# A state space layer over 24 chunks: other places in the order of work for its side matmuls and softplus, and five lent sum units instead of seven

## The chip, the cores and the metric

The kernel runs on one core of a Trainium2 chip. The time is that of one execution on the device, in microseconds (us), as the median of several runs. TensorE does the matmuls and the transposes, VectorE the scans and sums, ScalarE the activations, GpSimd elementwise work, and SyncE issues the DMAs. The engines run on their own and are ordered by semaphores; each engine works through its own list strictly in order.

## The reference, cut to what matters

Four layers follow one another on an input of 4 images, 384 channels, 48 x 48 pixels. Only the first, a state space block after a group norm, is touched. For each image, with L = 2304 pixels as a sequence:

```
xin, z = split(xn @ in_proj_w.T)                   # 768 + 768 channels
xin = silu(conv4(xin) + conv_b)                    # causal, 4 taps
dt, B, C = split(xin @ x_proj_w.T)                 # 24, 16, 16
dt = softplus(dt @ dt_proj_w.T + dt_proj_b)
h = exp(dt * A) * h + dt * B * xin                 # 16 states per channel, a scan along L
y = sum over states(h * C) + xin * D
out = layernorm((y * silu(z)) @ out_proj_w.T)
x = x + out
```

Layers 2 to 4 (an FFT convolution, a sparse 11 x 11 convolution, a gated mixture) are the same in both kernels.

## The kernel before, in words

**Chunks and units.** The sequence of each image is cut into 6 chunks of T = 384 pixels, so there are NCH = 24 chunks. Each chunk needs 96 scans of 384 pixels (16 states x 6 blocks of 128 channels); two share one scan instruction, so a chunk has PAIRS = 48 units. For a unit, TensorE transposes six 128 x 128 blocks of dt*B*x into PSUM (`inputs`, line 451, tiles pw0 and pw1 in turn), ScalarE computes two exponentials exp(dt*A) (line 600) and a copy of the start states (605), and VectorE scans (744). Three units make one state r. TensorE then transposes the states back, six blocks a unit, into the one tile pw2 (`turned`, 462), and VectorE adds them, weighted with C, to an accumulator a_acc (763; 757 for the first state). GpSimd prepares dt*B*x for three units at a time (`scaled`, 882) and keeps the last states (888).

**Lent units.** In the units that the tuple `LENT` names (positions 0 to 47 in a chunk), VectorE does not do the sum: ScalarE copies pw2, weighted, into a_tm12 (614), and GpSimd adds that to a_acc (894). The next `turned` waits until pw2 has been read, by VectorE or by ScalarE.

**Steps.** A chunk's main loop has STEPS = 96 steps n. In even steps are `inputs` and the scan of unit n/2, in odd ones `turned` and the sum of unit (n-1)/2 - 3. So the lent units 20, 22, 24, 26, 38, 41, 43 stand at the odd steps 47, 51, 55, 59, 83, 89, 93. ScalarE's exponentials run LEAD = 7 steps ahead; its lent copy is at the even step after.

**Side work.** Beside chunk k's main loop run chunk k-1's end (`post_*`: transposes of a_acc 344, gate, out-projection 353, layer norm, transposes G 360 and the residual 655) and chunk k+1's start (`pre_*`, `gate_*`: in-projections P 373 and Z 413, causal convolution, x-projection 381, B and C 387, the dt-projection V 394, softplus, transposes T 401). Each is a generator that yields the step at which its next piece is due; `march` issues what is due before the step's main work, in order of these times. On TensorE side work is issued only in odd steps, ahead of that step's `turned`. The times are written by hand: A_AT, O_AT (with O_GAP), LN_AT, G_AT, T_AT, Z_AT, and numbers in the functions. Chunk 0's start runs alone, before the first scan; the last chunk's end runs beside the next layer, with its times times 0.35.

**Banks.** Side matmuls write one of two PSUM banks: ps3 (`S`) or ps2 (`D`). `Turn.claim` makes each new user wait until the last one has been read. In the kernel before, P, B and C, V, T and Z all use S; the a_acc transposes, the out-projection, x-projection and G use D. V's reader on ScalarE is a pair, Abs into dt and Relu into raw (548, 549); then Exp and Ln run over all six blocks at once (552, 556: 128 x 2304), and GpSimd makes dt and dt*x (841, 845).

**DMA order.** SyncE's list has, for each chunk, the store of x of chunk k-1 (waits for the last G operation, v_g) and the reload of its buffer with chunk k+2. In the third chunk of images 0 to 2, VectorE also takes the statistics of the next image from 18 pieces that go through one buffer a_sx (705); 13 of their loads are issued before the store and the reload, 5 behind them.

Of the kernel before, what the change touches and what calls it, by code (L numbers as in the profile page):

```python
# [18 lines left out]
T = 384  # L19
# [344 lines left out]
def pre_pe(e, m, w, S, D, k):  # L364
    s, ps, pd, ident, o = m.s, m["ps3"], m["ps2"], m["g_ident"], k % 2
    for i in range(6):
        for kk in range(CT):
            yield 2.5 + 5.4 * i + 1.6 * kk
            if kk == 0:
                S.claim("a_raw", 6 * k + i + 1)  # L370
                w.wait_ge("p_xn", 3 * (k + 1))
                w.wait_ge("d_w0", 96)
            t = e.matmul(ps[:, 0:T], m["a_WinT"][:, kk, i * 128:(i + 1) * 128], m["a_xn"][:, kk, :], start=kk == 0, stop=kk == 2)  # L373
        t.then_inc(s["pe_P"], 1)
    for j in range(6):
# [48 lines left out]


def stats_pe(e, m, w, D, b):
    yield 89
    D.claim("v_st", GN * b + 24)
    w.wait_ge("v_st", GN * b + 23)
    w.wait_ge("d_c", 32)  # L430
    groups_pe(e, m, m["ps2"], m["a_mv"]).then_inc(m.s["pe_gn"], 1)


def l0_pe(e, m, w, S, D):
    s, ident = m.s, m["g_ident"]
    w.wait_ge("d_c", 32)
    march([stats_pe(e, m, w, D, 0)], 0)
    march([pre_pe(e, m, w, S, D, 0), gate_pe(e, m, w, S, 0)], 0)

    def inputs(k, p):  # L440

        pi = PAIRS * k + p
        g, c = NS * k + p // 3, 2 * (p % 3)
        ps = m[f"pw{pi % 2}"]
        w.wait_ge("p_dbt", g + 1)
        w.wait_ge("v_scan", pi - 1)
        w.wait_ge("v_w", 5)
# [49 lines left out]
def pre_act(e, m, w, k):  # L497
# [42 lines left out]
    for i in range(6):  # L540
        yield 58.4 + 0.8 * i
        w.wait_ge("pe_V", 6 * k + i + 1)
        w.wait_ge("p_cv", 24 * (k + 1))
        if k % NQ < NQ - 1:
            w.wait_ge("p_halo", k + 2)
        w.wait_ge("p_dtx", 6 * (k - 1))
        w.wait_ge("a_exp", 3 * PAIRS * (k - 1))
        e.activation(dt[:, i, :], ps[:, 0:T], ACT.Abs, bias=pv[:, i, 5:6])
        e.activation(raw[:, i, 3:T + 3], ps[:, 0:T], ACT.Relu, bias=pv[:, i, 5:6]).then_inc(s["a_v"], 1)
    yield 64.5  # L550
    w.wait_ge("a_v", 6 * (k + 1))
    e.activation(dt[:], dt[:], ACT.Exp, scale=-1.0).then_inc(s["a_sp"], 1)
    yield 67
    w.wait_ge("a_sp", 2 * k + 1)
    w.wait_ge("p_const", 3)
    e.activation(dt[:], dt[:], ACT.Ln, bias=m["a_one"][:, 0:1]).then_inc(s["a_sp"], 1)
# [74 lines left out]
def post_dve(e, m, w, k):  # L631
# [185 lines left out]
def pre_pool(e, m, w, k):  # L817
# [111 lines left out]
def l0_sp(e, m, d, w):  # L929
# [37 lines left out]

POST = 0.35
# [1213 lines left out]
```

## Time and profile before

| | us |
|---|---|
| median of 3 runs | 5353.92 (5347.02 to 5355.37) |
| the profiled execution | 5347.93, span 5346.1 |
| state space stage, first scan to last sum | 3210.2 |
| VectorE busy over the span | 4381.3 (82%) |
| TensorE busy over the span | 4686.3 (88%) |
| ScalarE, GpSimd busy over the span | 3070.4 (57%), 2970.7 (56%) |

All rows come from one execution; times are from the span's start. A row's length is that of the instruction; the next one on the same engine can start some 0.1 us before it ends, so what an instruction costs in a full row of work is the distance between starts. A value in brackets is the engine's idle time before it and what ended it. A 384-column matmul in fp32 shows as two instructions (x2), one transposed set as six. "PEclk" is the granted TensorE clock as a share of 2.4 GHz; 0.5 is its lower level, 1.2 GHz.

### The profile page before, as it was taken

Reading aid. Unit: us, or ns where it says so; the run is one execution under the profiler, and the core shown is the slowest. Engines: PE = TensorE matmul, PEld = TensorE weight load, DVE = VectorE, ACT = ScalarE, POOL = GpSimd, SP = SyncE. Lnnn points to the kernel's source line nnn. Section 1 sums busy time; section 2 is a strip of 40 time slices with the busy share of each in tenths; the row PEclk is TensorE's granted clock in tenths of the full one; section 3 lists DMA queues with packets and bytes.
Section 4 is the critical chain, followed back from the end, with each engine's and each line's share of the span. In section 5 each row is a group of like instructions: output and inputs, shape, how many; then the busy total and the mean of one; then the engine's idle time right before and its main releaser. Section 6 shows DMA issues by size and latency. Waiting matters only on the chain.

```text
span 5346.1 us, 78656 instructions
## 1 busy us (share of the span) xinstructions
PE 4686.3 (88%) x28623; PEld 3835.5 (72%) x28623; DVE 4381.3 (82%) x4965; ACT 3070.4 (57%) x6391; POOL 2970.7 (56%) x3552
## 2 busy tenths in 40 slices
PE   4888888888888888888888886779998899999999
PEld 2666666666666666666666665446877799999999
DVE  1999999999999999999999999677677765665555
ACT  3777777777777777777777774333332223333333
POOL 3776777777777777777777775456554520000000
PEclk8999999999999999999999999889797988999999
DMA  2001000001000001000000001110201021112110
GB/s 78 1 13 33 10 10 10 10 11 35 10 10 10 10 11 35 10 10 10 10 10 10 10 5 44 44 32 20 92 20 41 26 72 53 54 51 60 45 60 29
DMA packets 96933, 148.64 MB, mean 28 GB/s; under 512 B 5748, under 2 KB 93604, under 8 KB 96548
## 3 DMA queue, kind: packets, MB, share of 16 engines
q1 hardware_dynamic: 96548, 143.63, 8.4%
q8 instruction: 227, 3.72, 0.3%
q14 instruction: 158, 1.29, 0.1%
HBM read 101.00 MB, written 42.61 MB: 27 GB/s over the span
## 4 chain that ended last, share of the span: by engine, by line
PE 50%; issue 15%; DVE 15%; POOL 12%; ACT 7%; DMA 1%; POOLq 0%; DVEq 0%; SPq 0%; ACTq 0%
PE pw L1776 8%; PE pw L1763 6%; PE pw L462 6%; PE pw L451 6%; DVE a_h L744 5%; POOL a_dBT L882 4%; PE ps L413 3%; PE ps L353 3%; DVE b_cv L1393 3%; PE ps L373 2%; DVE a_acc L763 2%; PE ps L1763 2%; POOL a_xin L834 2%; POOL a_acc L894 2%; PE pw L1176 2%
## 5 line engine op out<-in xcount | busy, mean ns | idle before, releaser
L744 DVE TENSOR_TENSOR_SCAN a_h<-a_dA,pw 128x771 f32<-128x771 f32 x1152 | 2015.7, 1752 | 125.6 <-PE pw L451 124.6
L600 ACT ACTIVATE a_dA<-a_dt,a_Aneg 128x384 f32<-128x384 f32 x2304 | 1345.5, 607 | 155.0 <-DVE a_h L744 150.1
L462 PEld LDWEIGHTS pw<-g_ident,a_h 128*128 128x128 f32 x6912 | 786.6, 142 | 619.8 <-DVE a_acc L763 267.1
L882 POOL TENSOR_SCALAR a_dBT<-a_dtxT,a_BC 128x768 f32<-128x768 f32 x1152 | 1026.2, 909 | 300.7 <-PE pw L451 216.6
L462 PE MATMUL pw<-g_ident,a_h 128*128 128x128 f32 x6912 | 983.1, 279 | 227.5 <-DVE a_acc L763 158.1
L451 PE MATMUL pw<-g_ident,a_dBT 128*128 128x128 f32 x6912 | 958.9, 276 | 4.8 <-POOL a_dBT L882 4.8
L763 DVE SCALAR_TENSOR_TENSOR a_acc<-pw,a_BC,a_acc 128x768 f32<-128x768 f32 x912 | 915.3, 1004 | 52.5 <-PE pw L462 48.1
L451 PEld LDWEIGHTS pw<-g_ident,a_dBT 128*128 128x128 f32 x6912 | 806.5, 143 | 6.5 <-POOL a_dBT L882 5.5
L834 POOL TENSOR_TENSOR a_xin<-a_xin,a_tm 128x384 f32<-128x384 f32 x432 | 433.3, 1003 | 34.2 <-ACT a_tm L521 9.0
L1887 DVE TENSOR_TENSOR d_hf<-d_hf,d_wb 128x384 f32<-128x384 f32 x288 | 159.1, 557 | 312.4 <-ACT d_hf L1819 300.2
L894 POOL TENSOR_TENSOR a_acc<-a_acc,a_tm 128x768 f32<-128x768 f32 x168 | 307.4, 1830 | 171.1 <-ACT a_tm L614 170.2
L413 PE MATMUL ps<-a_xn,a_WinT 128*128 128x384 f32 x864 | 345.5, 502 | 30.7 <-ACT a_sz L577 15.1
L373 PE MATMUL ps<-a_xn,a_WinT 128*128 128x384 f32 x864 | 350.8, 490 | 10.2 <-ACT a_raw L509 5.1
L353 PE MATMUL ps<-a_WoT,a_sz 128*128 128x384 f32 x864 | 338.9, 489 | 23.1 <-POOL a_sz L793 23.1
L1819 ACT ACTIVATE d_hf<-pw,d_b 128x384 f32<-128x384 f32 x216 | 125.2, 580 | 352.0 <-PE pw L1763 352.0
L1279 ACT ACTIVATE b_xh<-ps 128x384 fp32r<-128x384 f32 x144 | 70.6, 490 | 415.5 <-PE ps L1132 415.5
L1776 PE MATMUL pw<-e_hh,c_W2h 128*128 128x384 f32 x864 | 288.8, 334 | 1.7 <-DVE e_hl L1892 1.7
L1776 PE MATMUL pw<-e_hl,c_W2h 128*128 128x384 f32 x864 | 288.6, 334 | 0.0
L1776 PE MATMUL pw<-e_hh,c_W2l 128*128 128x384 f32 x864 | 288.6, 334 | 0.0
L1591 POOL TENSOR_SCALAR b_xw<-b_x,b_sw,b_bw 128x384 f32<-128x384 f32 x288 | 223.1, 796 | 114.8 <-PE pw L1132 114.7
L1575 POOL TENSOR_TENSOR b_cv<-b_cv,b_tm 128x768 f32<-128x768 f32 x96 | 196.3, 2045 | 131.4 <-ACT b_tm L1260 127.0
L521 ACT ACTIVATE a_tm<-a_raw,a_pv 128x384 f32<-128x384 f32 x432 | 259.5, 601 | 7.4 <-POOL a_xin L834 7.3
(228 smaller groups left out, 9377.7 us busy)
## 6 DMA issues: line engine op xcount, KB each, us to landing
d_wb<-cw SPq DMA_DIRECT2D x24, 768.0 KB, 5.7
a_xs<-in_x SPq DMA_DIRECT2D x24, 576.0 KB, 3.9
x<-a_xs SPq DMA_DIRECT2D x24, 576.0 KB, 3.0
b_x<-x SPq DMA_DIRECT2D x24, 576.0 KB, 4.4
b_xs<-x SPq DMA_DIRECT2D x24, 576.0 KB, 5.0
e_xs<-x SPq DMA_DIRECT2D x24, 576.0 KB, 3.8
out<-e_xs SPq DMA_DIRECT2D x24, 576.0 KB, 5.8
a_sx<-in_x SPq DMA_DIRECT2D x54, 192.0 KB, 2.3
```

The lines of the kernel that those rows point to most:

```text
L353: t = e.matmul(pd[:, 0:C], m[f"a_sz{o}"][:, j, tb * 128:(tb + 1) * 128], m["a_WoT"][:, j, :], start=j == 0, stop=j == 5)
L373: t = e.matmul(ps[:, 0:T], m["a_WinT"][:, kk, i * 128:(i + 1) * 128], m["a_xn"][:, kk, :], start=kk == 0, stop=kk == 2)
L413: t = e.matmul(ps[:, 0:T], m["a_WinT"][:, kk, DI + i * 128:DI + (i + 1) * 128], m["a_xn"][:, kk, :], start=kk == 0, stop=kk == 2)
L451: t = e.transpose(ps[:, at:at + 128], m[f"a_dBT{g % 2}"][:, tb, (c + h) * 128:(c + h + 1) * 128], ident[:])
L462: t = e.transpose(m["pw2"][:, c * 128:(c + 1) * 128], m[f"a_h{g % 2}"][:, c // 2, first_col(c) + tb * 128:first_col(c) + (tb + 1) * 128], ...
L600: e.activation(dA[:, first_col(c):first_col(c) + T], m[f"a_dt{k % 2}"][:, c, :], ACT.Exp, scale=m["a_Aneg"][:, c, n:n + 1]).then_inc(s["a_ ...
L744: e.tensor_tensor_scan(m[f"a_h{g % 2}"][:, p % 3, :], m[f"a_dA{pi % NDA}"][:], m[f"pw{pi % 2}"][:, COL:COL + PAIR], 1.0, ALU.mult, ALU.add ...
L763: e.scalar_tensor_tensor(out=acc, in0=ps, scalar=cs, in1=acc, op0=ALU.mult, op1=ALU.add).then_inc(s["v_acc"], 1)
L834: e.tensor_tensor(xin[:, i, :], xin[:, i, :], m[f"a_tm{pr % NTM}"][:], ALU.add).then_inc(s["p_cv"], 1)
L882: t = e.tensor_scalar(m[f"a_dBT{g % 2}"][:, tb, :], m[f"a_dtxT{o}"][:, tb, :], m[f"a_BC{o}"][:, tb, n:n + 1], 1.0, ALU.mult, ALU.mult)
L1763: t = e.matmul(hidden3(m, hi), m[f"c_{A}"][:, kk, col], m[f"e_{B}{o}"][:, kk, :], start=kk == z == 0, stop=kk == z == 2)
L1776: t = e.matmul(ps, m[f"c_{A}"][:, i, col], m[f"e_{B}{u % 2}"][:, i, :], start=x == 0 and i == 0 and z == 0, stop=x == 3 and i == z == 2, s ...
```

## The change

- The times of TensorE's side work are written as slots, odd steps that hold at most about two matmuls; the due time says which. X-projection goes from 47 .. 53 to 48.5 .. 52.6, V is spread from 58 .. 62 to 56.6 .. 66.5, Z's eighteen matmuls get a time each, G moves from 60 .. 66 to 70.6 .. 84.7, and T from 78.6 .. 87.6 to 72.5 .. 84.6. The last out-projection block begins at 39.4 instead of 40.2.
- V, T and Z take the banks S and D in turn, as V_BANK, T_BANK and Z_BANK say.
- Softplus's Exp and Ln run on three blocks at a time, the first half between the two halves of V; GpSimd's dt and dt*x follow each half, from step 66 instead of 69.
- LENT has five units: 20, 26, 30, 38, 43, at the odd steps 47, 59, 67, 83, 93.
- In SyncE's list all 18 statistics loads stand before the store and the reload.

```
-O_AT, O_GAP, LN_AT = (18.8, 30, 40.2), (1.8, 1.6, 1.1), (29.5, 39.8, 47)
-G_AT = (60, 62.5, 66)
-T_AT = (78.6, 79.8, 81, 85.6, 86.6, 87.6)
-Z_AT = (63.5, 67.5, 71.5, 75, 82, 88.8)
-LENT = (20, 22, 24, 26, 38, 41, 43)
+O_AT, O_GAP, LN_AT = (18.8, 30, 39.4), (1.8, 1.6, 1.1), (29.5, 39.8, 46.6)
+X_AT = (48.5, 48.6, 50.5, 50.6, 52.5, 52.6)
+V_AT, V_BANK = (56.6, 58.5, 60.5, 64.5, 64.6, 66.5), "DSDDSD"
+Z_AT, Z_BANK = ((60.6, 62.5, 62.6), (68.5, 68.6, 70.5), (74.6, 76.5, 76.6), (78.5, 78.6, 80.5), (86.5, 86.6, 88.5), (90.5, 90.6, 92.5)), "SSDSSS"
+G_AT = (70.6, 80.6, 84.7)
+T_AT, T_BANK = (72.5, 72.6, 74.5, 82.5, 84.5, 84.6), "SDSSDS"
+SP_AT = (62.1, 68.1)
+DT_AT = (66, 67.9, 69.8, 71.7, 73.6, 75.5)
+LENT = (20, 26, 30, 38, 43)
...
     for j in range(6):                                        # pre_pe
-        yield 47 + 1.2 * j
+        yield X_AT[j]
...
-    yield 56.8
+    yield 56.5
     S.claim("a_bc", k + 1)
...
     for i in range(6):
-        yield 58 + 0.8 * i
-        S.claim("a_v", 6 * k + i + 1)
+        yield V_AT[i]
+        pi, bank = (ps, S) if V_BANK[i] == "S" else (pd, D)
+        bank.claim("a_v", 6 * k + i + 1)
...
-    yield 89                                                  # stats_pe
+    yield 88.6
...
-    yield 54.5                                                # pre_act
+    yield 53.5
...
+    for hf in range(2):
+        for i in range(3 * hf, 3 * hf + 3):
+            yield V_AT[i] + 0.9
+            ... Abs and Relu from the block's bank
+        half = dt[:, 3 * hf:3 * hf + 3, :]
+        yield SP_AT[hf]
+        w.wait_ge("a_v", 6 * k + 3 * hf + 3)
+        e.activation(half, half, ACT.Exp, scale=-1.0).then_inc(s["a_sp"], 1)
+        yield SP_AT[hf] + 1
+        w.wait_ge("a_sp", 4 * k + 2 * hf + 1)
+        e.activation(half, half, ACT.Ln, bias=m["a_one"][:, 0:1]).then_inc(s["a_sp"], 1)
     for u in range(6):
-        yield T_AT[u] + 0.4
+        yield T_AT[u] + 0.9
...
-        yield at + 3                                          # gate_act
+        yield Z_AT[i][2] + 0.9
...
-        yield G_AT[c] + 0.3                                   # post_dve
+        yield G_AT[c] + 0.8
-    yield 55.3                                                # pre_dve
+    yield 54.4
...
-        yield 69 + 2 * i                                      # pre_pool
-        w.wait_ge("a_sp", 2 * k + 2)
+        yield DT_AT[i]
+        w.wait_ge("a_sp", 4 * k + 2 * (i // 3) + 2)
...
-        for i in range(more - 5):                             # l0_sp
+        for i in range(more):
             stats(b + 1, i)
         if k > 0:
             store0(e, m, d, w, k - 1)
         if k + 2 < NCH:
             load(k + 2)
-        for i in range(max(0, more - 5), more):
-            stats(b + 1, i)
```

## Rows read from the trace of the kernel before

**Rows 1.** Stretches: us, busy (count) of PE PEld DVE ACT POOL, clock, DMA share, GB/s.
```profile
126.10:3336.30 3210.20, 2766.09 (x17863) 2127.84 (x17862) 3048.74 (x2588) 2387.49 (x5131) 2387.07 (x2965) 0.99 0.04 14
```

**Rows 2.** The same view with VectorE alone: chunks 1, 2, 3, 4.
```profile
246.90:379.90 133.00, 126.23 (x107) 0.99 0.03 11
379.90:523.90 144.00, 134.96 (x129) 0.96 0.11 32
523.90:658.40 134.50, 126.83 (x112) 0.99 0.03 10
658.40:789.70 131.30, 126.17 (x107) 1.00 0.03 10
```

**Rows 3.** Who waited for whom in chunk 12: us, times, longest.
```profile
DVE a_h L744 <- PE pw L451: 4.5, 3, 2.8
...
DVE a_acc L763 <- PE pw L462: 2.0, 5, 0.9
```

**Rows 4.** Timeline of VectorE in chunk 12: start, length, [idle before, releaser].
```profile
1801.27 1.76 DVE L744 TENSOR_TENSOR_SCAN a_h<-a_dA,pw 128x771 f32<-128x771 f32 x1 [2.85 <-PE pw L451]
1802.94 0.99 DVE L763 SCALAR_TENSOR_TENSOR a_acc<-pw,a_BC,a_acc 128x768 f32<-128x768 f32 x1
1803.85 1.75 DVE L744 TENSOR_TENSOR_SCAN a_h<-a_dA,pw 128x771 f32<-128x771 f32 x1
...
1847.65 3.47 DVE L744 TENSOR_TENSOR_SCAN a_h<-a_dA,pw 128x771 f32<-128x771 f32 x2
```

**Rows 5.** Timeline of TensorE in chunk 12.
```profile
1797.66 1.01 PE L381 MATMUL ps<-a_xin,a_WxT 128*128 128x384 f32 x2 [1.99 <-ACT a_ob L490]
1798.46 1.49 PE L462 MATMUL pw<-g_ident,a_h 128*128 128x128 f32 x6
...
1802.04 0.82 PE L462 MATMUL pw<-g_ident,a_h 128*128 128x128 f32 x6
...
1803.35 1.46 PE L381 MATMUL ps<-a_xin,a_WxT 128*128 128x384 f32 x4
1804.64 0.82 PE L462 MATMUL pw<-g_ident,a_h 128*128 128x128 f32 x6
...
1813.96 0.45 PE L394 MATMUL ps<-a_dt,a_Wdt 128*128 128x384 f32 x1 [1.14 <-ACT a_raw L549]
```

**Rows 6.** The view of stretches, columns as in rows 1: 3.4 us of chunk 12.
```profile
1799.00:1802.40 3.40, 3.40 (x17) 2.91 (x16) 1.13 (x1) 2.41 (x6) 2.08 (x3) 0.59 0.02 5
```

**Rows 7.** Timeline of ScalarE in chunk 12.
```profile
1797.15 0.47 ACT L490 ACTIVATE a_ob<-ps 128x384 f32<-128x384 f32 x1
...
1805.50 0.90 ACT L614 ACTIVATE a_tm<-pw,a_BC 128x768 f32<-128x768 f32 x1 [1.22 <-PE pw L462]
...
1821.54 0.58 ACT L548 ACTIVATE a_dt<-ps,a_pv 128x384 f32<-128x384 f32 x1
...
1822.48 1.12 ACT L600 ACTIVATE a_dA<-a_dt,a_Aneg 128x384 f32<-128x384 f32 x2
...
1823.59 2.12 ACT L552 ACTIVATE a_dt<-a_dt 128x2304 f32<-128x2304 f32 x1
```

**Rows 8.** One wait of VectorE between 400 and 3200 us.
```profile
DVE a_bn L705 <- DMA a_sx<-in_x: 12.0, 3, 4.1
```

**Rows 9.** Timeline before the first scan: ScalarE, GpSimd and VectorE.
```profile
92.29 0.58 ACT L548 ACTIVATE a_dt<-ps,a_pv 128x384 f32<-128x384 f32 x1 [0.78 <-PE ps L394]
...
101.75 0.86 POOL L841 TENSOR_TENSOR a_dt<-a_raw,a_dt 128x384 f32<-128x384 f32 x1 [28.28 <-ACT a_dt L556]
...
126.14 5.32 DVE L744 TENSOR_TENSOR_SCAN a_h<-a_dA,pw 128x771 f32<-128x771 f32 x3 [41.82 <-PE pw L451]
```

**Rows 10.** DMA issues of the page (KB each, us to landing), and SyncE's timeline.
```profile
a_xs<-in_x SPq DMA_DIRECT2D x24, 576.0 KB, 3.9
x<-a_xs SPq DMA_DIRECT2D x24, 576.0 KB, 3.0
...
3296.06 3.96 SPq L1652 DMA_DIRECT2D b_x<-x  x6
```

More of the change, by code:

```diff
@@ L389, in pre_pe @@
     for i in range(6):
-        yield 58 + 0.8 * i
-        S.claim("a_v", 6 * k + i + 1)
+        yield V_AT[i]
+        pi, bank = (ps, S) if V_BANK[i] == "S" else (pd, D)
+        bank.claim("a_v", 6 * k + i + 1)
         w.wait_ge("v_dt3", k + 1)
         w.wait_ge("v_w", 7)
-        e.matmul(ps[:, 0:T], m["a_Wdt3"][:, i * 128:(i + 1) * 128], m["a_dt3"][:], start=True, stop=True).then_inc(s["pe_V"], 1)
+        e.matmul(pi[:, 0:T], m["a_Wdt3"][:, i * 128:(i + 1) * 128], m["a_dt3"][:], start=True, stop=True).then_inc(s["pe_V"], 1)
     for hf in range(2):
@@ L397, in pre_pe, with gate_pe @@
             yield T_AT[3 * hf + tb]
-            S.claim("a_dtx", 6 * k + 3 * hf + tb + 1)
+            pi, bank = (ps, S) if T_BANK[3 * hf + tb] == "S" else (pd, D)
+            bank.claim("a_dtx", 6 * k + 3 * hf + tb + 1)
             w.wait_ge("p_dtx", 6 * k + 3 * hf + 3)
             for c in range(3):
-                t = e.transpose(ps[:, c * 128:(c + 1) * 128], m["a_raw"][:, 3 * hf + c, 3 + tb * 128:3 + (tb + 1) * 128], ident[:])
+                t = e.transpose(pi[:, c * 128:(c + 1) * 128], m["a_raw"][:, 3 * hf + c, 3 + tb * 128:3 + (tb + 1) * 128], ident[:])
             t.then_inc(s["pe_T"], 1)
-def gate_pe(e, m, w, S, k):
-    s, ps = m.s, m["ps3"]
-    for i, at in enumerate(Z_AT):
+def gate_pe(e, m, w, S, D, k):
+    s = m.s
+    for i in range(6):
+        ps, bank = (m["ps3"], S) if Z_BANK[i] == "S" else (m["ps2"], D)
         for kk in range(CT):
-            yield at + 1.3 * kk
+            yield Z_AT[i][kk]
             if kk == 0:
-                S.claim("a_sz", 6 * k + i + 1)
+                bank.claim("a_sz", 6 * k + i + 1)
                 w.wait_ge("p_xn", 3 * (k + 1))
@@ L437, in l0_pe @@
     march([stats_pe(e, m, w, D, 0)], 0)
-    march([pre_pe(e, m, w, S, D, 0), gate_pe(e, m, w, S, 0)], 0)
+    march([pre_pe(e, m, w, S, D, 0), gate_pe(e, m, w, S, D, 0)], 0)
     def inputs(k, p):
@@ L468, in l0_pe @@
         if k + 1 < NCH:
-            side += [pre_pe(e, m, w, S, D, k + 1), gate_pe(e, m, w, S, k + 1)]
+            side += [pre_pe(e, m, w, S, D, k + 1), gate_pe(e, m, w, S, D, k + 1)]
         if q == 3 and b + 1 < NB:
@@ L533, in pre_act @@
     e.activation(m["a_tm0"][32:64, :], pd[32:64, 0:T], ACT.Copy).then_inc(s["a_x"], 1)
-    yield 57.3
+    yield 57.4
     w.wait_ge("pe_BC", k + 1)
@@ L539, in pre_act @@
     dt = m[f"a_dt{o}"]
[L540 to L556, printed above, removed]
+    for hf in range(2):
+        for i in range(3 * hf, 3 * hf + 3):
+            yield V_AT[i] + 0.9
+            pi = ps if V_BANK[i] == "S" else pd
+            w.wait_ge("pe_V", 6 * k + i + 1)
+            w.wait_ge("p_cv", 24 * (k + 1))
+            if k % NQ < NQ - 1:
+                w.wait_ge("p_halo", k + 2)
+            w.wait_ge("p_dtx", 6 * (k - 1))
+            w.wait_ge("a_exp", 3 * PAIRS * (k - 1))
+            e.activation(dt[:, i, :], pi[:, 0:T], ACT.Abs, bias=pv[:, i, 5:6])
+            e.activation(raw[:, i, 3:T + 3], pi[:, 0:T], ACT.Relu, bias=pv[:, i, 5:6]).then_inc(s["a_v"], 1)
+        half = dt[:, 3 * hf:3 * hf + 3, :]
[4 more added lines that the diff above has]
+        w.wait_ge("a_sp", 4 * k + 2 * hf + 1)
+        w.wait_ge("p_const", 3)
+        e.activation(half, half, ACT.Ln, bias=m["a_one"][:, 0:1]).then_inc(s["a_sp"], 1)
     for u in range(6):
-        yield T_AT[u] + 0.4
+        yield T_AT[u] + 0.9
         w.wait_ge("pe_T", 6 * k + u + 1)
@@ L561, in pre_act @@
         hf, tb = divmod(u, 3)
-        e.activation(m[f"a_dtxT{o}"][:, tb, hf * T:(hf + 1) * T], ps[:, 0:T], ACT.Copy).then_inc(s["a_dtx"], 1)
+        e.activation(m[f"a_dtxT{o}"][:, tb, hf * T:(hf + 1) * T], (ps if T_BANK[u] == "S" else pd)[:, 0:T], ACT.Copy).then_inc(s["a_dtx"], 1)
 def silu_gate(e, m, w, k):
@@ L571, in gate_act @@
     s, o = m.s, k % 2
-    for i, at in enumerate(Z_AT):
-        yield at + 3
+    for i in range(6):
+        yield Z_AT[i][2] + 0.9
         w.wait_ge("pe_Z", 6 * k + i + 1)
@@ L576, in gate_act @@
         w.wait_ge("pe_O", 3 * (k - 1))
-        e.activation(m[f"a_sz{o}"][:, i, :], m["ps3"][:, 0:T], ACT.Copy).then_inc(s["a_sz"], 1)
+        e.activation(m[f"a_sz{o}"][:, i, :], m["ps3" if Z_BANK[i] == "S" else "ps2"][:, 0:T], ACT.Copy).then_inc(s["a_sz"], 1)
 def last_gate_act(e, m, w):
@@ L838, in pre_pool @@
     for i in range(6):
-        yield 69 + 2 * i
-        w.wait_ge("a_sp", 2 * k + 2)
+        yield DT_AT[i]
+        w.wait_ge("a_sp", 4 * k + 2 * (i // 3) + 2)
         e.tensor_tensor(dt[:, i, :], raw[:, i, 3:T + 3], dt[:, i, :], ALU.add).then_inc(s["p_dt"], 1)
-        yield 70 + 2 * i
+        yield DT_AT[i] + 1
         w.wait_ge("p_dt", 6 * k + i + 1)
```

## The prediction

> **What bounds the kernel now.** I read the stages first [rows 1]. The middle one, 3210.2 us, is the state space layer's 24 chunks; VectorE is busy in 3048.7 us of it, TensorE in 2766.1. The other layers (2009.8 us) are not touched except where the last chunk's tail runs in them. Then the chunks [rows 2]: a usual one takes 133.0 us and VectorE idles 133.0 - 126.2 = 6.8 us in it. So it is VectorE's work plus a few us of waits, and the change trades one for the other. I call a chunk's steps s0, w1, s2, ... : s is a scan, w a weighted sum, and w is missing where the unit is lent.
>
> The waits of one usual chunk [rows 3]: three times a scan for its transposed inputs, 4.5 us, five times a sum for its transposed states, 2.0. In the timeline [rows 4] the largest stands at s48: 2.85 us, right after the lent w47. The other two scans are s52 and s90, behind the lent w51 and w89, 1.7 together. The longest sum wait, 0.9, is w61 among the V products; the rest are small ones at w53, w75 and w85, and one in steps 18 to 32, 0.3 in a usual chunk, which the change doesn't touch.
>
> Why 2.85: the first x-projection matmul stands in slot 47 and waits 1.99 us for the copy of the out-projection [rows 5]; ScalarE reads that bank only at 1797.15 [rows 7], behind its exponentials. After that idle the granted clock is 0.59 over 3.4 us, mostly the 1.2 GHz level [rows 6], and six transposes take 1.49 us where they else take 0.82 [rows 5]. A chunk without the clock's fall (131.3 us, granted 1.00, idle 5.1 [rows 2]) idles 1.7 less than the usual one: the sets of transposes behind w47 and before s48 are 2 x 0.67 longer, so I put the fall at about 1.3.
>
> **Price of the two returned sums.** A sum starts 0.91 before the next scan [rows 4]. A scan starts 1.67 before the sum that follows it; of two scans without a sum between (3.47 for both, 1.75 for one) the second starts 1.72 after the first, 0.05 later. So 2 x (0.91 - 0.05) = 1.73 us a chunk, 24 chunks: +41.5 us of VectorE. ScalarE loses 2 x 0.80, GpSimd two adds; neither ends the chunk.
>
> **The slots.** An item due at t goes to the first odd step at or after t, before that step's transposes. On TensorE, six transposes of inputs, two 384-column matmuls and six of states take 1802.04 to 1804.64 = 2.60 us [rows 5]; VectorE's scan plus sum 1.67 + 0.91 = 2.58 [rows 4]. Two matmuls a unit thus just fit (steps 19 to 45 run so now, with the 0.3 of waits named above), and a lent unit (1.7 us against 1.31 of transposes) holds a third of one. Laid out slot by slot, the old lists overfill 47, 51, 59 and 89 (lent, two items each, 0.2 to 0.9 us too much); the new ones leave 47 empty, put one short item into 59, 67 and 83, one matmul into 93 as now, and never go over by more than 0.03 elsewhere (33, over by 0.7 in both, apart). By that count the waits at s48, s52, s90 and the small ones beside them go, some 5 us. For slot 47: the out-projection ends two steps earlier, its copy comes a step earlier, and x-projection stands in 49 behind it; what is late next is the lent copy of w47 (ScalarE's large Silu work ends shortly before), ending about 2.9 us after w45, with the transposes of w49 just in time: I leave 0.1.
>
> **ScalarE between 56 and 69** is what I do not get free. From the start of s56, VectorE would reach w69 after 7 scans and 4 sums, 7 x 1.67 + 4 x 0.91 = 15.3 us. For that the transposes have to start 0.9 before (state transposes 1802.04, sum 1802.94 [rows 4, 5]), and they wait for the lent copy of w67. ScalarE's work ahead of that copy's end: six V pairs at 0.94 (1821.54 to 1822.48) = 5.6, ten exponentials with their small copies 5 x 1.11 = 5.5, the first softplus half 2 x 1.11 = 2.2, two lent copies 2 x 0.80 = 1.6, a Z copy 0.4, BC 0.1: 15.4 us [rows 7]. It can start at -0.7 (V0 needs VectorE's correction in step 55) and has some 1.3 us of waits in between (step 59's exponential on s56, the copy of w59 on its transposes, V3 on its matmul). So the copy ends near +16.1, the transposes start at 16.3, w69 at 17.2: 1.8 us late, part of it showing at w65, where V4 waits for the Z copy on the same bank. Bounds: 0.4 (no waits inside the chain) to 4 (it starts 2 us late). I take 1.8. The softplus halves: by the rows a 1152-element pass lies between 0.61 (384) and 2.12 (2304), interpolated 1.21, less 0.1 overlap = 1.11, so four passes cost 0.4 more than two full ones.
>
> On the halves the Trainium skill (ScalarE: Activation LUTs, What ACT_TABLE_LOAD costs) states a fixed part per ACTIVATE, 186 ns with immediates and 93 more per pointer operand, less 93 of overlap; by it two more instructions cost an estimated 0.28 us a chunk where I interpolate 0.4. The rule speaks against splitting; no row of before has a half pass.
>
> **Slot 85** holds T4, T5 and G2, and T4 and G2 share a bank: G2 waits until ScalarE has copied T4, which is due in step 86, behind the lent copy of w83 and two exponentials. From w81's end: state transposes at 0.1, lent copy 1.0 to 1.8, exponentials to 2.9, T4's copy to 3.4, G2 to 3.8, w85 at 4.7; VectorE (one G operation 0.5, two scans) is there at 3.9. I add 0.8 us; bounds 0 and 1.6.
>
> So a usual chunk idles 0.3 + 0.1 + 1.8 + 0.8 + 0.1 = 3.1 us instead of 6.8.
>
> **The statistics chunks** (3 of 24, 144.0 us, idle 9.0 [rows 2]). Now SyncE issues 13 loads, then the store, which waits for G, and the reload, then 5 loads; VectorE waits 4 us for the 14th (12.0 in three [rows 8]), TensorE idles with it, the chunk's granted clock is 0.96 [rows 2], and some 2.8 us more go at w75 and its neighbours while it is low. With all 18 loads first both go, and the 18 extra VectorE operations give ScalarE time: idle about 2.5. Past them the queue has the store and the reload, which G at 85.5 makes later: v_g at about 86, store landing 3.0, load 3.9 [rows 10], so some 7.3 us later, near step 92; its user (xn, step 95) waits for the last Z matmul of slot 93 anyway. Cost 0; if the load were 2 us late it would eat ScalarE's lead and no VectorE time.
>
> **Sum.** Idle saved: 13 usual chunks x 3.7 = 48; 3 statistics chunks x 6.5 = 19.5; 3 after them (idle 7.7, to 3.3) 13; 3 more (5.1 to 3.1) 6; chunk 0 about 1; the last has no side work. 87.5 less 41.5 = 46 us. **Start**: before the first scan at 126.14 [rows 9] the six V products go back and forth on one bank at 1.83 us each (1.05 for the pair of reads, 0.78 of ScalarE's idle time); GpSimd starts only at 101.75, after the full softplus. With two banks and halves it starts near 90, the second half near 97, and the T and Z turns, alternating, end near 111.5 instead of 119.7. I take 8 us (bounds 4 and 10). **Hand-over**: G of chunk 22 moves by 19 steps, so the six loads of the next layer start at about 3321 instead of 3296 [rows 10]; with the weights behind them they take some 15 us, to about 3336, when the next layer begins: +0 to 3, taken as 0. Total: -54 us.
>
> The profiled execution took 5347.93 (span 5346.1 and 1.8 around it), 6.0 under the median 5353.92. 5348 - 54 = 5294, as a median 5300.
>
> **Rivals.**
> - *ScalarE keeps up* (w69 and w85 not late): 2.6 us less in 21 to 22 chunks, -56: 5244. For: ScalarE is busy only 2387.5 of the stage's 3210.2 us [rows 1]. Against: the chain above. 20%.
> - *The clock falls at the new waits.* At 69 and 85 TensorE idles 0.9 and 1.3 us. The one idle of a usual chunk after which the clock fell was 1.99; a gap of 1.14 left it [rows 5]. If it falls once a chunk, 1.3 us x 21 = +27: 5327. 13%. The Trainium skill (TensorE: Matmul & The Clock Gate, A second HAM failure mode: psum-queue depth-cycling) says that short idles from cycling through PSUM banks can make the clock swing; that is this case, and the trace's 1.1 us gaps so far do not bear it out.
> - *ScalarE falls behind at w67* (slower): V, Z and lent copies queue in order, each late copy holds a bank, TensorE waits with the transposes behind it, and the delay feeds itself. It decides from 54/23 = 2.35 us a chunk beyond my 1.8, a wait of 4.2 us at w69. With 3 us beyond: 5300 + 69 = 5369. For: the chain's slack is below zero; against: exponentials are issued seven steps ahead, so only the copies can be late. 10%.
> - *The wait at s48 stays*, because ScalarE's copies there are late whatever the slot: +2.7 x 21 = 57: 5357, no change. 7%.
>
> My forecast has 50%, with its own range 5275 to 5325. The median of such runs tells 0.2% (11 us): faster under 5343. Faster 0.50 + 0.20 + 0.13 less a little at the edges = 0.82; same 0.08; slower 0.10. Range 5235 to 5350: from under the first rival to just short of the fourth.
>
> **What would show it.** No idle over 0.3 us at s48, s52, s90 and no L381 wait on a_ob; granted clock 1.00 in usual chunks; 43 sums of 1.00 us a chunk; the two new waits at w65 to w69 (about 1.8) and w85 (0.8), released by TensorE behind ScalarE; chunks of 131.0 us; no wait on a_sx; the first scan near 118. I am wrong if idle per usual chunk is outside 1 to 5 us, or if the new clock falls appear in each chunk.

## The result, and the profile after

The changed kernel took 5271.14 us (median of 4 runs, 5267.32 to 5274.19), the kernel before on the same chip 5352.68 (4 runs, 5347.02 to 5355.37): ratio 0.9849, 95% interval 0.9832 to 0.9866, 81.5 us faster. The forecast was 5300 with a range of 5235 to 5350. The profiled execution after took 5274.19 (span 5272.4), the highest of its four, and that of before 5347.93, near its lowest, so between the two traces there are only 73.7 us.

First the view of stretches for the whole state space stage of the kernel after, to be laid beside [rows 1]:

```profile
118.00:3251.20 3133.20, 2711.41 (x17862) 2104.37 (x17861) 3073.11 (x2636) 2348.30 (x5129) 2298.11 (x2916) 1.00 0.05 14
```

The stage is 77 us shorter (3210.2 to 3133.2) although VectorE does 24 us more work in it. The same view with VectorE alone, chunks 1 to 4 (beside [rows 2]) and chunk 12:

```profile
238.30:368.00 129.70, 127.18 (x108) 1.00 0.04 12
368.00:504.70 136.70, 135.54 (x132) 1.00 0.12 34
504.70:635.50 130.80, 127.86 (x113) 1.00 0.03 10
635.50:765.30 129.80, 127.27 (x109) 1.00 0.03 10
1682.10:1811.90 129.80, 127.27 (x109) 1.00 0.03 10
```

A usual chunk went from 133.0 to 129.8 us: VectorE is busy 1.0 more, and its idle time fell from 6.8 to 2.5. The first statistics chunk went from 144.0 to 136.7, the one after it from 134.5 to 130.8. The granted clock is 1.00 (2.4 GHz) in each; it fell 19 times within chunks 1 to 22 of the kernel before and not once after.

What VectorE waited for between 400 and 3100 us (us in total, times, longest). This one line is the whole answer of the view: no scan waits for its transposed inputs now, and the wait for the statistics' DMA [rows 8] is gone.

```profile
DVE a_acc L773 <- PE pw L469: 46.1, 80, 1.1
```

VectorE in chunk 12, steps 65 to 70, then step 85 (beside [rows 4]; in brackets the idle time before and what ended it):

```profile
1771.18 1.02 DVE L773 SCALAR_TENSOR_TENSOR a_acc<-pw,a_BC,a_acc 128x768 f32<-128x768 f32 x1 [0.24 <-PE pw L469]
1772.11 3.53 DVE L754 TENSOR_TENSOR_SCAN a_h<-a_dA,pw 128x771 f32<-128x771 f32 x2
1776.76 1.02 DVE L773 SCALAR_TENSOR_TENSOR a_acc<-pw,a_BC,a_acc 128x768 f32<-128x768 f32 x1 [1.12 <-PE pw L469]
...
1798.39 1.02 DVE L773 SCALAR_TENSOR_TENSOR a_acc<-pw,a_BC,a_acc 128x768 f32<-128x768 f32 x1 [0.80 <-PE pw L469]
```

TensorE around the same three places (beside [rows 5]; L399 is V, L469 the state transposes, L364 G). At w65 a V product stands in front of the state transposes and has waited for the copy of Z on its bank; at w69 the transposes themselves wait for the lent copy of w67; at w85 the third G waits for the copy of T4:

```profile
1770.03 0.45 PE L399 MATMUL ps<-a_dt,a_Wdt 128*128 128x384 f32 x1 [1.14 <-ACT a_sz L587]
...
1775.85 0.88 PE L469 MATMUL pw<-g_ident,a_h 128*128 128x128 f32 x6 [0.71 <-ACT a_tm L624]
...
1797.16 0.55 PE L364 MATMUL ps<-g_ident,a_ob 128*128 128x128 f32 x3 [1.16 <-ACT a_dtxT L572]
```

ScalarE ahead of the w67 copy (1774.87), beside [rows 7]: the two reads of V5 stand right before it, and nothing here has an idle time in brackets.

```profile
1773.44 0.62 ACT L610 ACTIVATE a_dA<-a_dt,a_Aneg 128x384 f32<-128x384 f32 x1
1773.94 0.59 ACT L557 ACTIVATE a_dt<-ps,a_pv 128x384 f32<-128x384 f32 x1
1774.40 0.60 ACT L558 ACTIVATE a_raw<-ps,a_pv 128x384 f32<-128x384 f32 x1
1774.87 0.93 ACT L624 ACTIVATE a_tm<-pw,a_BC 128x768 f32<-128x768 f32 x1
```

Where the 73.7 us between the two traces are, by starts of scans: the first scan is 8.1 us earlier (118.0 for 126.1 [rows 9]); chunks 0 to 22 took 3000.0 us instead of 3079.5, 79.5 less; the last chunk 2.7 more, for its two further sums and a fallen clock in its last transposes; and from the last sum to the end 2021.2 instead of 2009.9, 11.3 more. The code of that last part differs only in the state space layer's tail. Over the fourteen traces of this study it varied between 2005.8 and 2023.7 us: the five whose last chunk has the old G times (before, e1, e2, e3, e8) took 2005.8 to 2016.0, mean 2011.8, the nine with the new ones 2010.8 to 2023.7, mean 2017.5. The two groups overlap, and kernels with the same tail differ by 10 to 13 us among themselves, so whether some 6 of the 11.3 us come from the change is not shown.

### The profile page after: what moved, and what is told of

Its sections match the earlier page's. It is cut to its first block, busy times and chain, and to the rows that moved or that the text cites. A ratio compares the mean times of both kernels' runs of the same rounds, so it can differ in the third digit from the quotient of the medians.

```text
span 5272.4 us, 78583 instructions
## 1 busy us (share of the span) xinstructions
PE 4648.9 (88%) x28623; PEld 3823.3 (73%) x28623; DVE 4407.9 (84%) x5013; ACT 3030.6 (57%) x6391; POOL 2881.8 (55%) x3504
## 4 chain that ended last, share of the span: by engine, by line
PE 42%; DVE 20%; issue 15%; ACT 13%; POOL 8%; DMA 0%; DVEq 0%; POOLq 0%; SPq 0%; ACTq 0%
DVE a_h L754 10%; PE pw L1784 9%; PE pw L1771 6%; ACT a_dA L610 5%; PE pw L469 4%; DVE a_acc L773 3%; PE ps L357 3%; PE pw L458 3%; DVE b_cv L1401 3%; PE ps L377 2%; POOL a_xin L844 2%; PE ps L1771 2%; PE pw L1184 2%; PE ps L1184 2%; POOL a_dBT L892 2%
## 5 line engine op out<-in xcount | busy, mean ns | idle before, releaser
L754 DVE TENSOR_TENSOR_SCAN a_h<-a_dA,pw 128x771 f32<-128x771 f32 x1152 | 2011.8, 1750 | 33.8 <-PE pw L458 33.4
L610 ACT ACTIVATE a_dA<-a_dt,a_Aneg 128x384 f32<-128x384 f32 x2304 | 1363.8, 612 | 353.8 <-DVE a_h L754 348.6
L469 PEld LDWEIGHTS pw<-g_ident,a_h 128*128 128x128 f32 x6912 | 772.1, 141 | 677.1 <-DVE a_acc L773 341.1
L469 PE MATMUL pw<-g_ident,a_h 128*128 128x128 f32 x6912 | 973.6, 277 | 295.9 <-DVE a_acc L773 225.9
L773 DVE SCALAR_TENSOR_TENSOR a_acc<-pw,a_BC,a_acc 128x768 f32<-128x768 f32 x960 | 960.8, 1001 | 57.3 <-PE pw L469 55.3
L458 PE MATMUL pw<-g_ident,a_dBT 128*128 128x128 f32 x6912 | 944.8, 273 | 4.8 <-POOL a_dBT L892 4.8
L458 PEld LDWEIGHTS pw<-g_ident,a_dBT 128*128 128x128 f32 x6912 | 793.4, 142 | 6.6 <-POOL a_dBT L892 5.4
L377 PE MATMUL ps<-a_xn,a_WinT 128*128 128x384 f32 x864 | 353.6, 494 | 8.9 <-POOL a_xn L865 5.0
L420 PE MATMUL ps<-a_xn,a_WinT 128*128 128x384 f32 x864 | 329.0, 492 | 2.4 <-ACT a_raw L558 1.0
L1401 DVE SCALAR_TENSOR_TENSOR b_cv<-b_ti,b_dw,b_cv 128x768 f32<-128x768 f32 x192 | 257.3, 1380 | 0.1
```

The source lines that it names most:

```text
L610: e.activation(dA[:, first_col(c):first_col(c) + T], m[f"a_dt{k % 2}"][:, c, :], ACT.Exp, scale=m["a_Aneg"][:, c, n:n + 1]).then_inc(s["a_ ...
L754: e.tensor_tensor_scan(m[f"a_h{g % 2}"][:, p % 3, :], m[f"a_dA{pi % NDA}"][:], m[f"pw{pi % 2}"][:, COL:COL + PAIR], 1.0, ALU.mult, ALU.add ...
L773: e.scalar_tensor_tensor(out=acc, in0=ps, scalar=cs, in1=acc, op0=ALU.mult, op1=ALU.add).then_inc(s["v_acc"], 1)
L1401: e.scalar_tensor_tensor(out=dst, in0=src, scalar=dw[:, o, k:k + 1], in1=dst, op0=ALU.mult, op1=ALU.add).then_inc(s["v_c"], 1)
```

## The experiments

Each is an edit of the kernel before or of the changed one, timed beside the kernel before on the same chip. Ratios are to the kernel before; the changed kernel's is 0.9849.

**Parts of the change, alone on the kernel before.**

*e1: five lent units alone.*

```
-LENT = (20, 22, 24, 26, 38, 41, 43)
+LENT = (20, 26, 30, 38, 43)
```

> The kernel before with the five lent units 20, 26, 30, 38, 43 and nothing else of the change. Theory (the slots brought the time, the returned sums cost it): two more sums a chunk at 0.86 us are +41 us; w51 and w89 are no longer lent, so the waits at s52 and s90 (0.55 + 0.2 + 1.1 us, some 22 chunks) go, -40; w67, newly lent behind two items and ScalarE's softplus, waits 1 to 2 us, +22 to +44. Sum: about 5375 us, slower than before by 0 to 1%. Rival (fewer lent units are by themselves the gain, because GpSimd and ScalarE are relieved): under 5340. In the trace the 2.85 us at s48 stays in either case.

Measured: 5397.3 us, ratio 1.0068 (1.0050 to 1.0087), usual chunk 133.4. The two returned sums with their new places, without the new slots, make the kernel 0.7% slower. s48 still waits (33.7 us in all), w69 now waits 36.5 in all, and the wait at s90 is gone but 13.6 stand at w89 in its place.

*e2: x-projection's slots and the out-projection's end.*

```
-O_AT, O_GAP, LN_AT = (18.8, 30, 40.2), (1.8, 1.6, 1.1), (29.5, 39.8, 47)
+O_AT, O_GAP, LN_AT = (18.8, 30, 39.4), (1.8, 1.6, 1.1), (29.5, 39.8, 46.6)
+X_AT = (48.5, 48.6, 50.5, 50.6, 52.5, 52.6)
-        yield 47 + 1.2 * j
+        yield X_AT[j]
```

> The kernel before with only the out-projection's third block at 39.4, the layer norm's at 46.6 and x-projection in the slots 49, 51, 53. Theory (the wait at s48 is x-projection standing before the transposes while its bank is unread): 2.75 us less in 19 chunks, 1.4 less in the three whose clock did not fall: -56 us, 5297; the granted clock stays at 1.00 through the usual chunks, and s52 still waits some 0.5 to 0.9 behind the lent w51. Rival (ScalarE is late there whatever the slot): within 10 us of before.

Measured: 5295.69 us, ratio 0.9879 (0.9862 to 0.9895). This alone is 1.2% of the change's 1.5%. The chunk is 130.0, the wait at s48 is gone and the clock falls 4 times instead of 19. What is left of the scans' waits, 400 to 3100 us, are s52 and s90, and the DMA wait still stands:

```profile
DVE a_h L745 <- PE pw L452: 31.1, 41, 1.5
DVE a_bn L706 <- DMA a_sx<-in_x: 12.0, 3, 4.1
```

*e3: all statistics loads first.* The edit is the last hunk of the diff.

> The kernel before with only SyncE's list changed, all 18 statistics loads ahead of the store and the reload. Theory (the fall of the clock is a consequence of the 4 us wait): the 4.0 and the 2.8 us go together in 3 chunks, -20 us, 5333, and the clock does not fall at step 70. Rival (the two are separate): -12 us, 5341, with the 2.8 us still at step 74 to 76.

Measured: 5331.02 us, ratio 0.9945 (0.9930 to 0.9960). The first statistics chunk fell from 144.0 to 136.2, at a granted clock of 1.00 where it was 0.96 [rows 2]:

```profile
382.36:518.56 136.20, 134.37 (x129) 1.00 0.12 34
```

The old order of the loads with the new steps of G was not tried: a load would stand behind a store that waits for G in step 85, while VectorE needs the piece in step 70 before it gets there, so by the order of the lists the kernel would hang.

**Parts of the change, taken back.**

*e4: the x-projection's and out-projection's old times in the changed kernel* (the edit of e2, reversed).

> The changed kernel with the out-projection, layer norm and x-projection back at the old times, so that two of their matmuls stand in the lent slot 47. Theory (this part carries the largest share of the gain): s48 waits 2.85 us where the clock falls and 1.5 where not, in 22 chunks: +33 to +60 us, 5305 to 5330. Rival (with the other slots in order the wait is absorbed later in the chunk): under 5285.

Measured: 5325.92 us, ratio 0.9934 (0.9914 to 0.9955), usual chunk 133.0; s48 waits 50.8 us in all again, the clock falls 13 times. The step is worth 0.9% on the changed kernel and 1.2% on the one before (e2).

*e6: V, T and Z all on bank S.*

```
-V_AT, V_BANK = (56.6, 58.5, 60.5, 64.5, 64.6, 66.5), "DSDDSD"
+V_AT, V_BANK = (56.6, 58.5, 60.5, 64.5, 64.6, 66.5), "SSSSSS"
(and T_BANK, Z_BANK likewise)
```

> The changed kernel with V, T and Z all on one bank, the slots as they are. Theory (turning banks removes waits of TensorE for a read just issued, wherever two items share a slot or follow closely): new waits of 0.3 to 1.1 us at w65 (V3, V4), w73 (T0, T1), w75 (T2, Z2), and the start of chunk 0 some 5 us later; +0.5 to +1.5 us a chunk, 5285 to 5310. Rival (the slots alone do it, the banks are for nothing but the start): 5271 to 5280.

Measured: 5369.3 us, ratio 1.0023 (1.0009 to 1.0038): by the ratios some 93 us over the changed kernel, where I had expected 15 to 40. So the slots and the five lent units without the second bank bring nothing. The first scan comes 12.9 us later (130.9), and the usual chunks take 132.7 or 134.3. The largest wait is at w61, 57.3 us over chunks 1 to 22, for a place I had left out: Z's first matmul in slot 61 stands ahead of the transposes and waits for the read of V2. TensorE in chunk 11 of this kernel, and below it 3.3 us of the view of stretches (columns as in [rows 1]):

```profile
1691.38 1.65 PE L420 MATMUL ps<-a_xn,a_WinT 128*128 128x384 f32 x2 [2.20 <-ACT a_raw L558]
1692.82 1.49 PE L469 MATMUL pw<-g_ident,a_h 128*128 128x128 f32 x6
1694.10 1.08 PE L458 MATMUL pw<-g_ident,a_dBT 128*128 128x128 f32 x6
```

```profile
1691.30:1694.60 3.30, 3.23 (x11) 2.51 (x12) 0.26 (x1) 3.30 (x6) 0.02 (x1) 0.50 0.00 0
```

After the 2.20 us the clock is at its 1.2 GHz level, and six transposes take 1.49 us again, as at s48 in the kernel before [rows 5, 6]. Usual chunks in which that happened took 134.3, the others 132.7.

*e7: one Exp and one Ln over all six blocks, at 69 and 70.*

```
-        half = dt[:, 3 * hf:3 * hf + 3, :]
-        yield SP_AT[hf]
...
+    yield SP_AT[1]
+    e.activation(dt[:], dt[:], ACT.Exp, scale=-1.0).then_inc(s["a_sp"], 1)
+    yield SP_AT[1] + 1
+    e.activation(dt[:], dt[:], ACT.Ln, bias=m["a_one"][:, 0:1]).then_inc(s["a_sp"], 1)
```

> The changed kernel with Exp and Ln over all six blocks at steps 69 and 70, GpSimd's work waiting for both. Theory (halves take 2.2 us out of ScalarE's chain behind... and let GpSimd start in time): the half is gone from the chain before the copy of w67, so the 1.1 us at w69 vanishes, but T0 in slot 73 then waits for GpSimd, which starts some 5 us late: 3 to 5 us a chunk between w73 and w79; net +2 to +4 a chunk and +4 at the start: 5320 to 5365. Rival (GpSimd's slack hides it): 5250, faster than the change.

Measured: 5519.21 us, ratio 1.0303 (1.0271 to 1.0335), chunk 140: 248 us over the changed kernel, where I had expected 50 to 95. I had counted one wait; there are two, in a row. GpSimd cannot make dt before the one Ln is done, its next dt*B*x stands behind that dt in its list, and the transposes of dt*x in slot 73, ahead of the state transposes of w73, wait for a dt*x that GpSimd gets to later still. TensorE, then VectorE, in chunk 12 of this kernel:

```profile
1915.06 1.54 PE L458 MATMUL pw<-g_ident,a_dBT 128*128 128x128 f32 x6 [4.92 <-POOL a_dBT L891]
...
1921.92 1.30 PE L407 MATMUL ps<-g_ident,a_raw 128*128 128x128 f32 x5 [5.32 <-POOL a_raw L854]
```

```profile
1916.64 1.76 DVE L753 TENSOR_TENSOR_SCAN a_h<-a_dA,pw 128x771 f32<-128x771 f32 x1 [4.63 <-PE pw L458]
1924.75 1.02 DVE L772 SCALAR_TENSOR_TENSOR a_acc<-pw,a_BC,a_acc 128x768 f32<-128x768 f32 x1 [6.35 <-PE pw L469]
```

So the halves save nothing by themselves (they cost ScalarE time); they are what lets T stand in slot 73. The changed kernel with full softplus and the old T times was not tried.

*e8: the last chunk's G at its old times.* Only the tail that runs into the next layer differs.

```
-        yield G_AT[c]
+        yield (G_AT if k < NCH - 1 else G_LAST)[c]        # G_LAST = (60, 62.5, 66)
```

> The changed kernel with the old G times for the last chunk alone, whose end runs beside the next layer. In the profiled runs the layers after the state space stage took 2021.2 us against 2009.9. Theory (that is where the clock happened to fall, not the change): within 0.15% of the changed kernel, 5264 to 5279, and the rest differs from run to run by some 10 us. Rival (the moved transposes and the later store disturb the next layer): 5260 or less, with a rest of 2010.

Measured: 5266.01 us, ratio 0.9830 (0.9802 to 0.9858). The last part took 2013.5 us in its trace, between the 2010 of the rival and the 2021 of the changed kernel. The intervals of the two kernels overlap for the most part; what the tail is worth, these runs can't tell.

**What the remaining 2.5 us are.**

*e5: w67 back on VectorE, four lent units.*

```
-LENT = (20, 26, 30, 38, 43)
+LENT = (20, 26, 38, 43)
```

> The changed kernel with four lent units, 20, 26, 38, 43: the sum w67 is VectorE's again. Theory (the 1.1 us wait of w69 is ScalarE's chain of V reads and softplus half in front of the lent copy): that wait and the 0.2 at w65 go with the copy, the sum costs 0.86, so a usual chunk takes 129.3 to 129.7 us against 129.7, and the whole 5262 to 5271: one more unit of work on the busiest engine for nothing. Rival (TensorE's slots 65 to 69 are too full, whoever sums): the wait stays and the sum adds to it, +20 us, 5291.

Measured: 5260.67 us, ratio 0.9822 (0.9795 to 0.9848). The wait at w69 is gone and comes back nowhere (w65 still waits 0.25, w85 0.81). VectorE over chunk 12 (columns as in the stretches above) is busy 0.6 us longer than in the changed kernel and the chunk is 0.5 shorter:

```profile
1677.10:1806.40 129.30, 127.91 (x109) 1.00 0.03 10
```

*e9: the read of V5 behind the lent copy.*

```
-            yield V_AT[i] + 0.9
+            yield V_AT[i] + 0.9 if i < 5 else 68.05
```

> The changed kernel, but ScalarE's read of the sixth bias matmul stands at 68.05 in its list in place of 68, so the lent copy of the sum of step 67 goes ahead of it. Theory: VectorE's 1.1 us a usual chunk ahead of the fold of step 69 is this copy standing behind that read (0.94 us); with the copy ahead of it the wait falls to about 0.2, VectorE gets back 0.9 less what it does not lose of overlap, some 20 us in all: about 5251, chunk near 128.9. Rival: the copy is late because ScalarE as a whole is behind there (the same work stands ahead of it, only in another order), so that the wait goes to the folds of steps 71 to 75 or to the Exp of the second half: 5265 to 5275, chunk 129.8.

Measured: 5271.24 us, ratio 0.9845 (0.9831 to 0.9860). My theory was wrong and the rival right: the wait at w69 did fall to 0.19, and 0.74 stands at w73 in its place, chunk 129.7. VectorE in chunk 12 of this kernel, and TensorE at slot 73:

```profile
1779.44 1.02 DVE L773 SCALAR_TENSOR_TENSOR a_acc<-pw,a_BC,a_acc 128x768 f32<-128x768 f32 x1 [0.19 <-PE pw L469]
...
1785.96 1.02 DVE L773 SCALAR_TENSOR_TENSOR a_acc<-pw,a_BC,a_acc 128x768 f32<-128x768 f32 x1 [0.74 <-PE pw L469]
```

```profile
1784.39 0.87 PE L407 MATMUL ps<-g_ident,a_raw 128*128 128x128 f32 x6 [2.05 <-ACT a_sz L587]
```

T's first transposes now wait for a Z copy that stands behind the softplus's second half. In the changed kernel ScalarE has no idle time from the start of s62 on for 18 us, to step 75, so another order of its list only moves the wait. Only less work there (e5) removes one. After the new idle of 2.05 us the clock also fell in 7 of the 22 chunks.

*e10: slot 85 without a shared bank.*

```
-G_AT = (70.6, 80.6, 84.7)
+G_AT = (70.6, 80.6, 84.4)
-T_AT, T_BANK = (72.5, 72.6, 74.5, 82.5, 84.5, 84.6), "SDSSDS"
+T_AT, T_BANK = (72.5, 72.6, 74.5, 82.5, 84.5, 86.4), "SDSSSS"
(Z_BANK "SSDSSS" becomes "SSDSDS")
```

> The changed kernel, but the third gate matmul is issued at 84.4 ahead of the fifth time-step matmul, the sixth time-step matmul moves to slot 86, and the two swap banks with the fifth output matmul, so that no two matmuls of slot 85 share a bank. Theory: the 0.8 us a usual chunk ahead of the sum of step 85 is TensorE's stand for that bank; it goes in 22 chunks, 16 us in all: about 5255, chunk near 129.0; up to 3 us of it may come back where the statistics matmul of step 88 finds the same bank. Rival: the sum of step 85 is late because three matmuls stand in two slots whatever their banks: the wait stays or moves to step 87, 5268 to 5275.

Measured: 5274.36 us, ratio 0.9850 (0.9835 to 0.9865), again the rival. w85 waits no more, but w87 waits 0.64: Z4, now on bank D, stands there until VectorE has read the third G, a read that is in VectorE's list behind w85. TensorE in slot 87:

```profile
1801.16 1.56 PE L420 MATMUL ps<-a_xn,a_WinT 128*128 128x384 f32 x4 [1.22 <-DVE a_xs L665]
```

A usual chunk is 0.15 us shorter, but the first one after the statistics went from 130.8 to 133.0, with a wait of 1.6 at w89 and a fallen clock, and so did the other two; that took more than the usual chunks had won (chunks 0 to 22: 3003.7 against 3000.0).

*e11: e9 and e10 together.*

> The two edits together (the read of the sixth bias matmul at 68.05, and slot 85 with banks that differ). Theory: the two waits are independent, the sum of both gains: about 5236, chunk near 128.1, no wait of VectorE over 0.3 us left in a usual chunk. Rival: ScalarE is the next bound, some 1.2 us a chunk behind VectorE's work, and takes half of the gain back: 5250 to 5256.

Measured: 5270.41 us, ratio 0.9842 (0.9826 to 0.9859), chunk 129.5. Both expectations missed: two waits moved, none removed.

*e12: four lent units and the slot 85 of e10.*

> The sum of step 67 back on VectorE (four lent units a chunk) and slot 85 with banks that differ. Theory: the version with four lent units took 5260.7 and still waited 0.75 us a usual chunk ahead of the sum of step 85; without that, 5244, chunk near 128.6. If the lent copy can be moved instead of given back, the version with both edits and five lent units is some 8 us faster than this one; if ScalarE is the bound, this one is the faster.

Measured: 5262.25 us, ratio 0.9827 (0.9813 to 0.9842), not the 5244 that rested on e10's theory. It repeats e5: chunks 0 to 22 took 2992.8 us here and 2991.3 in e5, against 3000.0 in the changed kernel and 3006.3 in e11. The five lent units with both moves are not 8 us faster than four but 8 slower, as the last sentence of the expectation has it for a full ScalarE. Four lent units (5260.67, 5262.25) are the best found: 9 and 7 us less than the changed kernel over these chunks, 10 and 9 in the medians. The ratios' intervals overlap that of the changed kernel, so the times alone don't show it; the traces do, with 129.3 (e5) and 129.1 (e12) us in nearly every usual chunk against 129.7 or 129.8.

## Why the prediction was right, and where its sizes were off

**The direction and the mechanism held; the size was too small.** Forecast were 54 us, measured 81.5 (73.7 between the traces). The stage is VectorE's work plus its waits. The waits at s48, s52, s90, w61 and w75 went, no x-projection matmul waits on a_ob, and idle per usual chunk is 2.5 us, inside the 1 to 5 set. e2 and e4 show from both sides that the out-projection's copy ahead of x-projection was the largest part.

**Price of the two sums: 1.73 forecast, 1.04 measured** as VectorE's busy time per usual chunk (127.27 less 126.23). The sums are there (960 + 72 in 24 chunks, 43 each) and last 1.00 us. This term was the most mis-sized, because I took busy and idle time as separate terms. A scan or sum starts 0.08 us before its predecessor ends; after a wait it can't, and a sum after a wait is also 0.02 to 0.03 longer (1.02 for 0.99). In chunk 12 the kernel before had 8 waits [rows 3], the changed one 4: 0.4 of the 0.7. The rest I can't place, beyond that scans and sums are on average 2 to 3 ns shorter after, some 0.2 us a chunk, of which a part is the same thing. In e1, where a usual chunk still has 7 waits, the same two sums added 1.6 to VectorE's busy time.

**ScalarE from 56 to 69: 1.8 forecast, 1.36 measured** (1.12 at w69, 0.24 at w65), released as told in both places. The chain has less slack to lose than I counted; e5 confirms that the lent copy is it.

**Slot 85: 0.8 forecast, 0.80 measured**, behind the third G, which waits for the copy of T4 as told. The bounds were 0 and 1.6, so the exact hit is luck. **Softplus halves:** they last 1.16 and 1.25 us where I interpolated 1.21; on average 1.178 and 1.266 against 2.121 and 2.207, so four passes cost 0.56 more, less two overlaps of 0.1: near 0.36, where I took 0.4. The estimate by the Trainium skill (ScalarE: Activation LUTs, What ACT_TABLE_LOAD costs) was 0.28; the measurement lies above it.

**Statistics chunks: 4.8 us net forecast, 7.3 measured;** they idle 1.2 us, not 2.5, because the 18 extra VectorE operations give ScalarE time at w69 too (0.7 there). The ones after them: 2.7 forecast, 3.4 measured on average. e3 shows 7.8 for the load order alone, as [rows 2, 8] gave it.

**The start: 8 forecast, 8.1 measured**, and so near by luck: the four kernels with the old start (before, e1 to e3) have their first scan at 126.1 to 129.4, the eight with the changed kernel's start (after, e4, e5, e8 to e12) at 116.8 to 118.2, on average 10.6 us apart. GpSimd begins at 91.09 instead of 101.75:

```profile
91.09 0.86 POOL L851 TENSOR_TENSOR a_dt<-a_raw,a_dt 128x384 f32<-128x384 f32 x1 [15.74 <-ACT a_dt L566]
118.02 3.41 DVE L754 TENSOR_TENSOR_SCAN a_h<-a_dA,pw 128x771 f32<-128x771 f32 x2 [32.96 <-PE pw L458]
```

It takes both parts: with halves on one bank the first scan is at 130.92 (e6), with two banks and the full softplus at 126.41 (e7), neither earlier than in the kernel before:

```profile
130.92 1.76 DVE L754 TENSOR_TENSOR_SCAN a_h<-a_dA,pw 128x771 f32<-128x771 f32 x1 [46.68 <-PE pw L458]
126.41 1.76 DVE L753 TENSOR_TENSOR_SCAN a_h<-a_dA,pw 128x771 f32<-128x771 f32 x1 [42.80 <-PE pw L458]
```

**The hand-over: taken as 0; no DMA wait came, but 0 is not shown.** The last store and the next layer's loads came late, as told, and the weights behind them were issued by 3243; the layer's first matmul began at 3251.3, right after the last sum. What followed was 11.3 us longer, with the granted clock at its lower level for 295 us of it after and 263 before; as said above, a part of that may be the change's.

```profile
3231.88 0.37 SPq L936 DMA_DIRECT2D x<-a_xs  x1
3232.50 4.03 SPq L1660 DMA_DIRECT2D b_x<-x  x6
...
3242.75 0.58 SPq L1677 DMA_DIRECT2D b_dw<-in_dw  x1
```

**The sum.** For chunks 0 to 22 it comes to 47.7 us (46, and 1.7 for the last chunk, which only pays); measured 79.5, so 31.8 more. Of these 13 usual chunks bring 1.3 each (0.7 from the price of the sums, 0.4 from w65 to w69, the rest in small waits), 16.6; the statistics chunks 2.6 each, 7.9; the ones after them 0.8 each, 2.4; the three after those, 131.3 to 129.8 where I had 131.0, 1.2 each, 3.5; chunk 0 some 1.3. In the traces 1.0 of the last chunk and the 11.3 of the last part go against it: 54 + 31.8 + 0.1 - 1.0 - 11.3 = 73.6. The chunks' gain was thus forecast at 0.6 of what it was, and the last part hid a third of the miss.

**The rivals.** ScalarE kept up better than forecast, but not wholly, and 5271 lies between my forecast (5300) and the first rival (5244), just below the 5275 to 5325 that I gave the forecast by itself. The clock did not fall at the waits of 1.1 and 1.2 us; where it does fall, it costs a usual chunk 1.6 to 1.7 (133.0 against 131.3 in [rows 2]), not the 1.3 of that rival. The Trainium skill (TensorE: Matmul & The Clock Gate, A second HAM failure mode: psum-queue depth-cycling) tells of short idles from cycling through PSUM banks that make the clock swing. Here the runs point the other way: with banks in turn it did not fall in 22 chunks, with the one bank of e6 it fell eleven times, each at the end of an idle of 2.2 us or up to 1.4 us behind it. ScalarE did not fall behind for good at w67, but e9 shows how full it is; s48 did not stay.

## What to carry to other kernels

A matmul in a strictly ordered list that waits for a slow reader holds everything behind it; move it past its reader before saving any work elsewhere. When an engine shows no idle time in a stretch, expect another order of its list only to move the wait: e9 moved one from w69 to w73 and won nothing, while taking 0.8 us of work off that engine (e5) shortened the chunk by 0.4, even at the price of a sum on the bounding engine. e10 moved a wait in the same way on a shared bank. A split that costs time where it stands can still be needed, for what it lets start earlier (e7). And when a wait goes, count the overlap that comes back with it.

## What the runs showed of the hardware that was not expected

- **Which idles the clock survives.** Over chunks 1 to 22 of the six traces that I counted (before, after, e6, e7, e9, e10), TensorE's idles of 1.0 to 1.7 us were never followed within 5 us by a fall of the granted clock; those near 2.0 us were in 16 of 19 cases before but only 7 of 22 in e9 (and 4 of 19 in e1); those of 2.2 us in 11 of 22 in e6; those over 4 us in all three cases before, and e7, with two of them a chunk, had a fall in each of the 22 chunks. At 2 us the size alone does not decide, and a fall can come without a long idle before it: e10's three falls have nothing larger than 0.58 in the 5 us before them, and one of the nine in e1, which is not among the six, nothing larger than 1.14. Their cause stays open.
- **What a fall costs** can be read from like chunks of one trace: 134.3 against 132.7 us in e6, 133.0 against 131.3 in the kernel before, so 1.6 to 1.7 us.
- **What a wait costs beyond itself:** about 0.1 us of VectorE, the overlap of 0.08 and 0.02 to 0.03 of a longer next sum. e9, with one wait more in a usual chunk than the changed kernel, is busy 0.1 longer in it (127.3 against 127.2); e4's further wait at s48 does not show in this way (127.2), so it is not the same at every place.
